# One PSUM bank for each evicting engine in the layer norm's transposes of an eight-core transformer and expert layer

## The chip, the cores and the metric

The kernel runs on the 8 cores of one Trainium2 chip. Each core does the whole program on a sequence of 2048 tokens of its own, with the same weights, and the cores exchange nothing. The time is the device time of the slowest core in microseconds (us), as a median of several runs.

## What is computed

The input is 8 x 2048 x 1024 in float32, 1024 being the width. Four transformer blocks run in turn, each with a layer norm, an attention half and a second layer norm with an FFN of width 4096. Of the eight heads four attend in windows of 128 tokens, and four are causal linear attention in buckets of 64. After them comes a sum with the input, a plain layer norm, and a dense mixture of 64 experts of width 512 with a shared one, then a last layer norm.

```python
for i in range(DEPTH):                       # 4
    x = x + self_attention(layer_norm(x, ln1_g[i], ln1_b[i]), Wq[i], Wk[i], Wv[i], Wo[i], bo[i])
    h = layer_norm(x, ln2_g[i], ln2_b[i])
    x = x + (gelu(h @ W1[i] + b1[i]) @ W2[i] + b2[i])
...
x = _layernorm(x0 + x)
shared = silu(xf @ Ws_up) @ Ws_down
h = silu(einsum('td,edf->etf', xf, W_up))
y = einsum('etf,efd->etd', h, W_down)
routed = einsum('etd,te->td', y, cw)         # cw: weights of the 8 chosen of 64 experts, else 0
out = _layernorm(x + shared + routed)
```

## The kernel before, in words

The activations stay in SBUF all the time: x_sb holds the 16 token blocks of 128 tokens by 1024 in float32. Matmuls want the activations transposed, with the width on the partitions. So each layer norm writes its result as bfloat16 into aT, transposed, and the stage behind it reads aT.

emit_ln makes one such layer norm. It is called nine times: two for each of the four blocks, and one before the experts. It has two parts. The first takes the variances of all 16 token blocks, ACT and DVE in turn (L308, L317), and then the square root and the reciprocal on small tiles. The second is a loop over the 16 token blocks. In it, one engine normalises a block from x_sb into one half of apre: ACT for even blocks (L352), DVE for odd ones (L356). In the ninth call the same engine writes x_sb too, in place (L363 on ACT, L367 on DVE). TensorE transposes the block in 8 pieces of 128 x 128 into PSUM (L379). ACT and DVE then carry the 8 pieces from PSUM to aT, which is called eviction here. They apply the norm's gain and offset on the way (L401 on ACT, L405 on DVE); the ninth call has none and copies (L396, L398). A piece fills a quarter kilobyte per partition, 8 fill one PSUM bank. Block b uses bank 6 for even b and bank 7 for odd b, and piece dt is evicted by ACT for even dt and by DVE for odd dt.

The order of work is that in which the Python code emits it: each engine has its own queue in that order, and semaphores between engines are set by hand. Each engine counts its marks on one semaphore: s_te for TensorE, s_act, s_dve. A Guard protects a buffer or a bank: use(eng) makes an engine wait for the last mark of every engine that has used it, its own too, and done(eng) records its mark. There is one Guard for each PSUM bank (gbank), one for aT (gaT), and those of apre (gapre and one for each eighth of it). A wait that the engine has already made for as high a count is left out.

Around the norms: before each norm the POOL queue waits for TensorE's last mark, and then issues the weight loads of the next stage as soon as their slots are free. emit_attention and emit_ffn start with a matmul that waits for aT_toks, the marks behind the last evictions. Banks 6 and 7 are used elsewhere only by attention, for small transposes (L655, L894). The other six banks (Pf) take the matmuls.

Of the kernel before, what the change touches and what calls it, by code (L numbers as in the profile page):

```python
# [38 lines left out]
class Eng:  # L39
    def __init__(self, bass_eng, sem, name):  # L40
        self.e = bass_eng
        self.sem = sem
        self.name = name
        self.count = 0
        self.waited = {}
        self.last_inst = None
        self.last_tok = None
# [71 lines left out]
class Guard:  # L119

    def __init__(self, prog):
        self.p = prog
        self.marks = {}

    def use(self, eng):
        for name, tok in list(self.marks.items()):
            self.p.wait(eng, tok)

    def done(self, eng):
        self.marks[eng.name] = eng.mark()  # L130

    def done_tok(self, name, tok):
        self.marks[name] = tok


def build_program(n_layers=DEPTH, do_top=True, do_moe=True, n_experts=NE,
# [31 lines left out]
    with ExitStack() as stack:  # L168
# [16 lines left out]
        te, act, dve, sp, gp = P.te, P.act, P.dve, P.sp, P.gp  # L185

        gbank = [Guard(P) for _ in range(8)]
# [20 lines left out]
        def stage_use_all(eng):  # L208
            gstage.use(eng)
            for n in SREGS:  # L210
                RG(n).use(eng)
# [6 lines left out]
        def apre_use_half(eng, half):  # L218
            gapre.use(eng)
            for i in range(4 * half, 4 * half + 4):  # L220
                apg(i).use(eng)

        def apre_done_half(eng, half):
            tok = eng.mark()
            gapre.done_tok(eng.name, tok)
            for i in range(4 * half, 4 * half + 4):
                apg(i).done_tok(eng.name, tok)
# [14 lines left out]
        def fpair(i, n=1024):  # L242
            return Pf[:, i * 512:i * 512 + n]

        def bbank(i, lo=0, hi=1024):
            return Pb[:, (i - 6) * 1024 + lo:(i - 6) * 1024 + hi]

        def sm(col, n=1):
            return smalls[:, col:col + n]

        def xt(t, lo=0, hi=1024):
            return x_sb[:, t * 1024 + lo:t * 1024 + hi]

        def aTv(dt, t0, t1):
            return aT[:, dt * T + t0:dt * T + t1]
# [41 lines left out]
        def emit_ln(gcol, bcol, sums_toks, inplace_nat=False, gb_toks=()):  # L297
            P.waits(dve, sums_toks)
            dve.emit(nc.vector.tensor_scalar(
                sm(NEGMU, NT), sm(SUMS, NT), -1.0 / D, None, op0=ALU.mult))  # L300
            negmu_tok = dve.mark()
            P.wait(act, negmu_tok)
            for t in range(NT):
                engv = act if t % 2 == 0 else dve
                if engv is act:
                    stage_use_all(engv)
                    P.wait(engv, xw_tok[t])
                    engv.emit(nc.scalar.activation(  # L308
                        stage[:], xt(t), AF.Square, bias=sm(NEGMU + t),
                        scale=1.0, accum_out=sm(VARSS + t)))  # L310
                    gstage.done(engv)
                else:
                    gbank[0].use(engv)
                    gbank[1].use(engv)
                    P.wait(engv, xw_tok[t])
                    P.wait(engv, negmu_tok)
                    engv.emit(nc.vector.scalar_tensor_tensor(  # L317
                        fpair(0), xt(t), sm(NEGMU + t), xt(t),
                        op0=ALU.add, op1=ALU.mult,
                        accum_out=sm(VARSS + t)))  # L320
                    gbank[0].done(engv)
                    gbank[1].done(engv)
            vs_tok = act.mark()
            P.wait(dve, vs_tok)
            P.selfbar(dve)
            dve.emit(nc.vector.tensor_scalar(
                sm(STD, NT), sm(VARSS, NT), 1.0 / D, 1e-5,
                op0=ALU.mult, op1=ALU.add))
            pre_tok = dve.mark()
            P.wait(act, pre_tok)  # L330
            act.emit(nc.scalar.activation(sm(STD, NT), sm(STD, NT), AF.Sqrt))
            std_tok = act.mark()
            P.wait(dve, std_tok)
            dve.emit(nc.vector.reciprocal(sm(RECR, NT), sm(STD, NT)))
            P.selfbar(dve)
            dve.emit(nc.vector.tensor_tensor(
                sm(MUR, NT), sm(NEGMU, NT), sm(RECR, NT), op=ALU.mult))
            mur_tok = dve.mark()

            aT_toks = []  # L340
            tr_prev = {6: None, 7: None}
            for b in range(NT):
                t = b
                pb = 6 + (b % 2)
                half = b % 2
                ap0 = half * 1024
                neng = act if b % 2 == 0 else dve
                apre_use_half(neng, half)
                P.wait(neng, mur_tok)
                P.wait(neng, xw_tok[t])  # L350
                if neng is act:
                    neng.emit(nc.scalar.activation(  # L352
                        apre[:, ap0:ap0 + 1024], xt(t), AF.Identity,
                        bias=sm(MUR + t), scale=sm(RECR + t)))
                else:
                    neng.emit(nc.vector.tensor_scalar(  # L356
                        apre[:, ap0:ap0 + 1024], xt(t),
                        sm(NEGMU + t), sm(RECR + t),
                        op0=ALU.add, op1=ALU.mult))
                if inplace_nat:  # L360
                    P.selfbar(neng)
                    if neng is act:
                        neng.emit(nc.scalar.activation(  # L363
                            xt(t), xt(t), AF.Identity,
                            bias=sm(MUR + t), scale=sm(RECR + t)))
                    else:
                        neng.emit(nc.vector.tensor_scalar(  # L367
                            xt(t), xt(t), sm(NEGMU + t), sm(RECR + t),
                            op0=ALU.add, op1=ALU.mult))
                    xw_tok[t] = neng.mark()  # L370
                apre_done_half(neng, half)
                norm_tok = neng.mark()
                g = gbank[pb]
                g.use(te)
                apre_use_half(te, half)
                P.wait(te, norm_tok)
                P.wait(te, tok_cst)
                for dt in range(8):
                    te.emit(nc.tensor.transpose(  # L379
                        bbank(pb, dt * 128, (dt + 1) * 128),  # L380
                        apre[:, ap0 + dt * 128:ap0 + (dt + 1) * 128],
                        ident))
                g.done(te)
                apre_done_half(te, half)
                tr_tok = te.mark()
                for dt in range(8):
                    eng = act if dt % 2 == 0 else dve
                    g.use(eng)
                    gaT.use(eng)
                    P.wait(eng, tr_tok)  # L390
                    P.waits(eng, gb_toks)
                    src = bbank(pb, dt * 128, dt * 128 + 128)
                    dst = aTv(dt, t * 128, (t + 1) * 128)
                    if gcol is None:
                        if eng is act:
                            eng.emit(nc.scalar.copy(dst, src))  # L396
                        else:
                            eng.emit(nc.vector.tensor_copy(dst, src))  # L398
                    else:
                        if eng is act:  # L400
                            eng.emit(nc.scalar.activation(  # L401
                                dst, src, AF.Identity,
                                bias=sm(bcol + dt), scale=sm(gcol + dt)))
                        else:
                            eng.emit(nc.vector.tensor_scalar(  # L405
                                dst, src, sm(gcol + dt), sm(bcol + dt),
                                op0=ALU.mult, op1=ALU.add))
                    g.done(eng)
                aT_toks.append(act.mark())
                aT_toks.append(dve.mark())  # L410
            return aT_toks
# [787 lines left out]
        if do_top:  # L1199
# [26 lines left out]
            if do_moe:  # L1226
                cw_toks = []
                for t in range(NT):
                    pb = 2 + t % 2
                    g = gbank[pb]  # L1230
# [50 lines left out]
                for idx, eix in enumerate(ex_list):  # L1281
# [8 lines left out]
                    for fs in range(4):  # L1290
                        for tc in range(4):
                            pb = (fs * 4 + tc) % 2
                            g = gbank[pb]
# [24 lines left out]
                    for t in range(NT):  # L1318
# [8 lines left out]
                        for half in range(2):  # L1327
                            pbk = pair + half
# [186 lines left out]
```

How the kernel before makes its waits and increments, by code:

```python
    def mark(self):  # L49
        if self.last_tok is not None:
            return self.last_tok
        if self.last_inst is None:
            return None
        try:
            self.last_inst.then_inc(self.sem, 1)
        except Exception:
            self.e.maybe_drain_then_inc((self.sem, 1))
        self.count += 1
        self.last_tok = (self.sem, self.count, self)
        return self.last_tok
# [25 lines left out]
    def wait(self, eng, tok):  # L86
        if tok is None:
            return
        sem, val, owner = tok
        key = id(sem)
        if eng.waited.get(key, -1) >= val:
            return
        eng.e.wait_ge(sem, val)
        eng.waited[key] = val
# [8 lines left out]
    def dma(self, queue_eng, kind, out_ap, in_ap, deps=()):  # L103
# [4 lines left out]
        sem = pool["sems"][idx]  # L108
        prior = pool["uses"][idx]
        if prior:
            self.wait(queue_eng, (sem, 16 * prior, None))
        inst = queue_eng.e.dma_start(out_ap, in_ap)
        inst.then_inc(sem, 16)
        pool["uses"][idx] = prior + 1
        queue_eng.emit(inst)
# [20 lines left out]
def build_program(n_layers=DEPTH, do_top=True, do_moe=True, n_experts=NE,  # L136
# [1305 lines left out]
                P.dma(sp, "o", xvv, xv)  # L1442
            elif tn == "qkvA":
                P.dma(sp, "o", ap, qkvA[:])
            elif tn == "smalls":
                P.dma(sp, "o", ap, smalls[:])
        for kind in ("w", "x", "o"):
            pool = P.pools[kind]
            for sem, uses in zip(pool["sems"], pool["uses"]):
                if uses:
                    sp.e.wait_ge(sem, 16 * uses)
    return nc
```

## Time and profile before

| what | value |
|---|---|
| median of the 3 runs | 9803.64 us (9411.13 to 10576.59) |
| time of the profiled execution | 9405.97 us |
| its span (slowest core) | 9404.9 us; all cores 9392.5 to 9404.9 |
| PE busy | 7248.0 us, 77% of the span |
| DVE busy | 3433.5 us, 37% |
| ACT busy | 2298.1 us, 24% |
| granted TensorE clock, mean | 0.859 to 0.861 on all cores |

The span runs from the first to the last instruction of one profiled execution. Busy time is the sum of an engine's instructions. A released instruction shows, in square brackets, how long its engine stood idle before it and whose end let it go. The granted clock is a share of 2.4 GHz: 0.50 is 1.2 GHz.

### The profile page before, as it was taken

The page shows a single profiled execution, that of the slowest core. Times are in us where ns is not written, and L with a number is a line of the kernel's source. Part 1 is how long each engine was busy: PE and PEld are TensorE (multiplying, and loading weights), DVE is VectorE, ACT ScalarE, POOL GpSimd, SP SyncE. Part 2 cuts the span into 40 slices and gives each one's busy share as a digit, 9 for nine tenths or more (in the row PEclk, how much of TensorE's full clock was granted, in tenths as well). Part 3 has the DMA queues.
Part 4 walks back from the last instruction along what each step waited for, and adds up shares of the span by engine and source line. Part 5 has one row for each costly group of instructions (what it writes and reads, how often), then busy time and mean ns, then how long its engine had stood idle before and what let it go on. Part 6 is the DMA issues. An engine that isn't in the chain of part 4 may idle for free.

```text
span 9404.9 us, 113236 instructions; the slowest of 8 cores (9392.5 to 9404.9 us)
## 1 busy us (share of the span) xinstructions
PE 7248.0 (77%) x36528; PEld 3413.1 (36%) x36528; DVE 3433.5 (37%) x6712; ACT 2298.1 (24%) x5374; POOL 223.8 (2%) x275
## 2 busy tenths in 40 slices
PE   2555994565966557955559919999999999999996
PEld 1342432332423433423424314444444444444442
DVE  3443333432334333334433333333333333333333
ACT  2343223333123332233432121111111111111112
POOL 0000000000000000000000000000000000000000
PEclk9666996667987668976569959999999999999998
DMA  3001211001210011211012112222222222222221
GB/s 59 8 8 18 36 26 16 10 6 29 39 21 10 12 19 23 32 18 13 8 21 36 29 41 36 36 37 40 36 36 40 37 36 37 41 36 36 40 37 45
DMA packets 234511, 269.89 MB, mean 29 GB/s; under 512 B 41824, under 2 KB 174048, under 8 KB 233952
## 3 DMA queue, kind: packets, MB, share of 16 engines
q0 software_dynamic: 224112, 237.14, 16.9%
q1 hardware_dynamic: 9840, 25.51, 0.8%
q8 instruction: 325, 5.32, 0.2%
q14 instruction: 234, 1.92, 0.1%
HBM read 491.36 MB, written 8.39 MB: 53 GB/s over the span
## 4 chain that ended last, share of the span: by engine, by line
PE 72%; DVE 9%; ACT 8%; issue 7%; DMA 2%; DVEq 1%; ACTq 0%; SPq 0%; POOLq 0%
PE Pf L1330 19%; PE Pf L1300 19%; PE Pf L1138 9%; PE Pf L1103 9%; PE Pf L1051 3%; ACT aT L401 3%; PE Pf L533 2%; PE Pf L851 2%; DVE aT L405 2%; PE Pf L500 2%; PE Pb L379 2%; PE Pf L790 2%; DVE stage L609 1%; ACT apre L884 1%; ACT apre L352 1%
## 5 line engine op out<-in xcount | busy, mean ns | idle before, releaser
L1353 DVE SCALAR_TENSOR_TENSOR x_sb<-Pf,smalls,x_sb 128x1024 f32<-128x1024 f32 x1024 | 1314.1, 1283 | 2320.0 <-PE Pf L1330 2318.2
L1330 PE MATMUL Pf<-wA,bigB 128*128 128x512 bf16 x8320 | 1826.5, 378 | 68.4 <-ACT bigB L1309 65.0
L1300 PE MATMUL Pf<-aT,wA 128*128 128x512 bf16 x8320 | 1808.2, 379 | 1.0 <-ACT bigB L1309 1.0
L1309 ACT ACTIVATE bigB<-Pf 128x512 bf16<-128x512 f32 x1040 | 620.8, 597 | 3038.9 <-PE Pf L1300 3038.9
L1300 PEld LDWEIGHTS Pf<-aT,wA 128*128 128x128 bf16 x8320 | 814.4, 98 | 983.8 <-issue 3.6
L1330 PEld LDWEIGHTS Pf<-wA,bigB 128*128 128x128 bf16 x8320 | 744.7, 97 | 1150.2 <-issue 393.1
L1138 PE MATMUL Pf<-wA,bigB 128*128 128x512 bf16 x4096 | 911.8, 379 | 36.1 <-ACT bigB L1114 34.9
L1165 DVE TENSOR_TENSOR x_sb<-Pf,x_sb 128x1024 f32<-128x1024 f32 x448 | 548.6, 1225 | 1052.3 <-PE Pf L1138 1051.2
L1103 PE MATMUL Pf<-aT,wA 128*128 128x512 bf16 x4096 | 897.0, 381 | 19.3 <-DVE aT L405 17.9
L379 PE MATMUL Pb<-constsB,apre 128*128 128x128 bf16 x1152 | 145.7, 307 | 993.8 <-ACT apre L352 477.9
L1114 ACT ACTIVATE bigB<-Pf,smalls 128x512 bf16<-128x512 f32 x512 | 351.5, 687 | 1337.2 <-PE Pf L1103 1337.2
L1103 PEld LDWEIGHTS Pf<-aT,wA 128*128 128x128 bf16 x4096 | 401.9, 98 | 508.9 <-issue 31.3
L1138 PEld LDWEIGHTS Pf<-wA,bigB 128*128 128x128 bf16 x4096 | 369.5, 97 | 545.6 <-issue 189.6
L379 PEld LDWEIGHTS Pb<-constsB,apre 128*128 128x128 bf16 x1152 | 111.5, 138 | 1027.9 <-issue 1027.9
L405 DVE TENSOR_SCALAR aT<-Pb,smalls 128x128 bf16<-128x128 bf16 x512 | 176.0, 344 | 569.7 <-ACT aT L401 569.7
L401 ACT ACTIVATE aT<-Pb,smalls 128x128 bf16<-128x128 bf16 x512 | 234.1, 457 | 479.8 <-PE Pb L379 248.2
L894 PE MATMUL Pb<-constsB,apre 128*128 128x128 bf16 x256 | 66.4, 259 | 310.3 <-ACT apre L884 310.3
L655 PE MATMUL Pb<-constsB,apre 128*128 128x128 bf16 x496 | 88.6, 277 | 266.5 <-DVE smalls L637 244.5
L500 PE MATMUL Pf<-wA,aT 128*128 128x256 bf16 x2048 | 278.5, 289 | 19.9 <-DVE aT L405 17.9
L1051 PE MATMUL Pf<-wA,bigB 128*128 128x512 bf16 x1024 | 251.5, 390 | 2.4 <-ACT bigB L968 2.4
L851 PE MATMUL Pf<-wA,aT 128*128 128x128 bf16 x2048 | 231.9, 302 | 27.5 <-DMA wA<-Wq 27.5
L790 PE MATMUL Pf<-wA,aT 128*128 128x256 bf16 x1024 | 178.1, 333 | 96.6 <-DVE qkvA L817 75.0
(122 smaller groups left out, 4829.4 us busy)
## 6 DMA issues: line engine op xcount, KB each, us to landing
wA<-W POOLq DMA_DIRECT2D x64, 1024.0 KB, 10.5
wA<-Wup POOLq DMA_DIRECT2D x64, 1024.0 KB, 10.8
wA<-Wdn POOLq DMA_DIRECT2D x64, 1024.0 KB, 9.8
x_sb<-x SPq DMA_DIRECT2D x1, 8192.0 KB, 35.3
wA<-Wv POOLq DMA_DIRECT2D x16, 512.0 KB, 7.6
wA<-Wo POOLq DMA_DIRECT2D x4, 2048.0 KB, 27.0
stage<-x SPq DMA_DIRECT2D x16, 512.0 KB, 3.5
out<-stage SPq DMA_DIRECT2D x16, 512.0 KB, 2.6
```

The source lines that it names most:

```text
L379: te.emit(nc.tensor.transpose(bbank(pb, dt * 128, (dt + 1) * 128), apre[:, ap0 + dt * 128:ap0 + (dt + 1) * 128], ident))
L401: eng.emit(nc.scalar.activation(dst, src, AF.Identity, bias=sm(bcol + dt), scale=sm(gcol + dt)))
L500: te.emit(nc.tensor.matmul(fbank(pb, 0, 256), aTv(dt, t * 128, (t + 1) * 128), wv(base + dt * 256, 256), start=(dt == 0), stop=(dt == 7)))
L851: te.emit(nc.tensor.matmul(fbank(pb, 0, 128), aTv(dt, t * 128, (t + 1) * 128), wv(qbase + dt * 256 + hh * 128, 128), start=(dt == 0), stop ...
L1051: te.emit(nc.tensor.matmul(fbank(pbk), oTv(et, t * 128, (t + 1) * 128), wv(6144 + et * 1024 + half * 512, 512), start=(et == 0), stop=False))
L1103: te.emit(nc.tensor.matmul(fbank(pb), wv(par * 4096 + dt * 512 + fs * 128, 128), aTv(dt, tc * 512, (tc + 1) * 512), start=(dt == 0), stop= ...
L1138: te.emit(nc.tensor.matmul(fbank(pbk), bigB[:, par * 8192 + fs * 2048 + t * 128: par * 8192 + fs * 2048 + (t + 1) * 128], wv(8192 + par * ...
L1165: dve.emit(nc.vector.tensor_tensor(xt(t), fpair(pair), xt(t), op=ALU.add))
L1300: te.emit(nc.tensor.matmul(fbank(pb), wv(par * 4096 + dt * 512 + fs * 128, 128), aTv(dt, tc * 512, (tc + 1) * 512), start=(dt == 0), stop= ...
L1309: act.emit(nc.scalar.activation(bigB[:, par * 8192 + fs * 2048 + tc * 512: par * 8192 + fs * 2048 + (tc + 1) * 512], fbank(pb), AF.Silu))
L1330: te.emit(nc.tensor.matmul(fbank(pbk), bigB[:, par * 8192 + fs * 2048 + t * 128: par * 8192 + fs * 2048 + (t + 1) * 128], wv(8192 + par * ...
L1353: dve.emit(nc.vector.scalar_tensor_tensor(xt(t), fpair(pair), sm(CW + t * 64 + eix), xt(t), op0=ALU.mult, op1=ALU.add, **kw))
```

## The change

The second part of emit_ln changes. Each token block now uses both banks: pieces 0 to 3 go into bank 6 and are all evicted by ACT, pieces 4 to 7 go into bank 7 and are all evicted by DVE. Each bank has the Guard it had. TensorE uses both Guards before a block's transposes and marks both behind them, and an evicting engine uses only the Guard of its own bank. The class Guard also gets a second kind of use, for readers, with use_r and done_r; no call of these two is in the kernel.

```diff
@@ class Guard
         self.marks = {}
+        self.readers = {}
 
     def use(self, eng):
-        for name, tok in list(self.marks.items()):
+        for tok in list(self.marks.values()):
+            self.p.wait(eng, tok)
+        for tok in list(self.readers.values()):
             self.p.wait(eng, tok)
 
     def done(self, eng):
         self.marks[eng.name] = eng.mark()
+        self.readers.clear()
...
@@ emit_ln
-                g = gbank[pb]
-                g.use(te)
+                g6 = gbank[6]
+                g7 = gbank[7]
+                g6.use(te)
+                g7.use(te)
                 apre_use_half(te, half)
                 P.wait(te, norm_tok)
                 P.wait(te, tok_cst)
                 for dt in range(8):
+                    pbk = 6 + (dt >= 4)
                     te.emit(nc.tensor.transpose(
-                        bbank(pb, dt * 128, (dt + 1) * 128),
+                        bbank(pbk, (dt % 4) * 128, (dt % 4 + 1) * 128),
                         apre[:, ap0 + dt * 128:ap0 + (dt + 1) * 128],
                         ident))
-                g.done(te)
+                g6.done(te)
+                g7.done(te)
                 apre_done_half(te, half)
                 tr_tok = te.mark()
                 for dt in range(8):
-                    eng = act if dt % 2 == 0 else dve
+                    eng = act if dt < 4 else dve
+                    g = g6 if dt < 4 else g7
                     g.use(eng)
                     gaT.use(eng)
                     P.wait(eng, tr_tok)
                     P.waits(eng, gb_toks)
-                    src = bbank(pb, dt * 128, dt * 128 + 128)
+                    src = bbank(6 + (dt >= 4), (dt % 4) * 128,
+                                (dt % 4) * 128 + 128)
                     dst = aTv(dt, t * 128, (t + 1) * 128)
```

No engine gets another instruction or another order of them; the waits change. The first place is DVE in the first norm, from the evictions of block 0 through the normalisation of block 1 to its evictions. L405 is the eviction, L356 the normalisation; each row ends with the semaphores that its instruction waits for. Before:

```order
L405 TENSOR_SCALAR aT<-Pb,smalls 128x128 [waits s_te,s_act,s_xdma3,s_xdma4]
L405 TENSOR_SCALAR aT<-Pb,smalls 128x128 [waits s_act,s_dve] x3
L356 TENSOR_SCALAR apre<-x_sb,smalls 128x1024
L405 TENSOR_SCALAR aT<-Pb,smalls 128x128 [waits s_te,s_act]
L405 TENSOR_SCALAR aT<-Pb,smalls 128x128 [waits s_act,s_dve] x3
```

The same place on DVE after the change, where the two lines are L423 and L368:

```order
L423 TENSOR_SCALAR aT<-Pb,smalls 128x128 [waits s_te,s_xdma3,s_xdma4]
L423 TENSOR_SCALAR aT<-Pb,smalls 128x128 [waits s_dve] x3
L368 TENSOR_SCALAR apre<-x_sb,smalls 128x1024 [waits s_act]
L423 TENSOR_SCALAR aT<-Pb,smalls 128x128 [waits s_te,s_dve]
L423 TENSOR_SCALAR aT<-Pb,smalls 128x128 [waits s_dve] x3
```

The wait for ACT has left the evictions, and one for ACT stands at the normalisation, where there was none; on ACT's queue the same holds the other way round.

The second place is PE at the transposes of the first three token blocks. Before:

```order
L379 MATMUL Pb<-constsB,apre 128x128 [waits barrier_Pool_Activation_PE_DVE_SP_release,s_act,s_xdma0]
L379 MATMUL Pb<-constsB,apre 128x128 x7
L379 MATMUL Pb<-constsB,apre 128x128 [waits s_te,s_dve]
L379 MATMUL Pb<-constsB,apre 128x128 x7
L379 MATMUL Pb<-constsB,apre 128x128 [waits s_act,s_te]
```

After, where the line is L394:

```order
L394 MATMUL Pb<-constsB,apre 128x128 [waits barrier_Pool_Activation_PE_DVE_SP_release,s_act,s_xdma0]
L394 MATMUL Pb<-constsB,apre 128x128 x7
L394 MATMUL Pb<-constsB,apre 128x128 [waits s_te,s_act,s_dve]
L394 MATMUL Pb<-constsB,apre 128x128 x7
L394 MATMUL Pb<-constsB,apre 128x128 [waits s_te,s_act,s_dve]
```

From the second block on, the first transpose waits for both ACT and DVE, where it waited for one of them in turn.

## Rows read from the trace of the kernel before

**Rows 1.** The page, busy tenths of PE in 40 equal slices of the span.

```profile
PE   2555994565966557955559919999999999999996
```

**Rows 2.** The page, groups by line: busy us, mean ns | idle before, releaser.

```profile
L405 DVE TENSOR_SCALAR aT<-Pb,smalls 128x128 bf16<-128x128 bf16 x512 | 176.0, 344 | 569.7 <-ACT aT L401 569.7
L401 ACT ACTIVATE aT<-Pb,smalls 128x128 bf16<-128x128 bf16 x512 | 234.1, 457 | 479.8 <-PE Pb L379 248.2
```

**Rows 3.** Line L379: idle time of PE before it, by what ended it (us, times).

```profile
  ACT apre L352: 477.9, 64
  DVE apre L356: 330.6, 64
  ACT x_sb L363: 147.6, 8
  DVE x_sb L367: 37.7, 8
```

**Rows 4.** Timeline, two token blocks of the second norm: start us, us, instruction [idle <-releaser].

```profile
839.47 1.01 PE L379 MATMUL Pb<-constsB,apre 128*128 128x128 bf16 x8 [5.08 <-ACT apre L352]
840.58 0.46 ACT L401 ACTIVATE aT<-Pb,smalls 128x128 bf16<-128x128 bf16 x1 [1.36 <-PE Pb L379]
...
841.58 0.46 ACT L401 ACTIVATE aT<-Pb,smalls 128x128 bf16<-128x128 bf16 x1 [0.54 <-DVE aT L405]
842.21 0.34 DVE L405 TENSOR_SCALAR aT<-Pb,smalls 128x128 bf16<-128x128 bf16 x1 [0.73 <-ACT aT L401]
842.65 0.46 ACT L401 ACTIVATE aT<-Pb,smalls 128x128 bf16<-128x128 bf16 x1 [0.61 <-DVE aT L405]
...
844.35 0.34 DVE L405 TENSOR_SCALAR aT<-Pb,smalls 128x128 bf16<-128x128 bf16 x1 [0.73 <-ACT aT L401]
844.61 0.80 DVE L356 TENSOR_SCALAR apre<-x_sb,smalls 128x1024 bf16<-128x1024 f32 x1
...
845.56 1.01 PE L379 MATMUL Pb<-constsB,apre 128*128 128x128 bf16 x8 [5.08 <-DVE apre L356]
...
849.81 0.46 ACT L401 ACTIVATE aT<-Pb,smalls 128x128 bf16<-128x128 bf16 x1 [0.61 <-DVE aT L405]
850.17 1.23 ACT L352 ACTIVATE apre<-x_sb,smalls 128x1024 bf16<-128x1024 f32 x1
...
851.65 1.01 PE L379 MATMUL Pb<-constsB,apre 128*128 128x128 bf16 x8 [5.08 <-ACT apre L352]
```

**Rows 5.** Timeline, PE's first matmuls of the FFN behind that norm.

```profile
924.17 2.29 PE L1103 MATMUL Pf<-aT,wA 128*128 128x512 bf16 x5 [4.47 <-DVE aT L405]
```

**Rows 6.** Timeline, linear attention: DVE waits for itself, ACT reads PSUM beside it.

```profile
456.50 0.28 DVE L979 TENSOR_TENSOR stage<-Pf,stage 128x129 f32<-128x129 f32 x1
456.51 0.21 ACT L968 CAST bigB<-Pf 128x64 bf16<-128x64 f32 x1 [0.61 <-PE Pf L957]
...
456.88 0.15 DVE L983 TENSOR_SCALAR smalls<-stage 128x1 f32<-128x1 f32 x1
```

**Rows 7.** Line L979, all its instructions: min/median/max ns, first and last start.

```profile
L979 DVE TENSOR_TENSOR stage<-Pf,stage x496: 272/293/296, 406.0 to 4733.7; 128x129 f32<-128x129 f32 x166
```

**Rows 8.** Timeline, one token block of the ninth norm.

```profile
5507.55 0.27 ACT L396 COPY aT<-Pb 128x128 bf16<-128x128 bf16 x1 [3.29 <-PE Pb L379]
...
5509.72 0.27 ACT L396 COPY aT<-Pb 128x128 bf16<-128x128 bf16 x1 [0.48 <-DVE aT L398]
5509.88 1.24 ACT L352 ACTIVATE apre<-x_sb,smalls 128x1024 bf16<-128x1024 f32 x1
5510.16 0.23 DVE L398 COPY aT<-Pb 128x128 bf16<-128x128 bf16 x1 [0.52 <-ACT aT L396]
5511.22 1.24 ACT L363 ACTIVATE x_sb<-x_sb,smalls 128x1024 f32<-128x1024 f32 x1
```

**Rows 9.** DMA from 811 to 925: busy tenths of the 16 engines in 40 slices.

```profile
DMA  1999999997400000000000000000000000000000
```

**Rows 10.** Busy us (x) of PE, PEld, DVE, ACT, POOL, PEclk, DMA share, GB/s, second norm.

```profile
829.00:918.00 89.00, 14.16 (x112) 10.85 (x112) 25.80 (x68) 34.86 (x66) 0.00 (x0) 0.50 0.14 22
```

More of the change, by code:

```diff
@@ L130, in done, with use_r, done_r @@
         self.marks[eng.name] = eng.mark()
+        self.readers.clear()
     def done_tok(self, name, tok):
         self.marks[name] = tok
+        self.readers.clear()
+    def use_r(self, eng):
+        for tok in list(self.marks.values()):
+            self.p.wait(eng, tok)
+    def done_r(self, eng):
+        self.readers[eng.name] = eng.mark()
 def build_program(n_layers=DEPTH, do_top=True, do_moe=True, n_experts=NE,
```

## The prediction

> **What bounds the kernel now.** Begin with how busy TensorE is along the span [rows 1]. PE is at 9 tenths in the expert stage and in the four FFN stages, and low between them. In some of the low slices it does next to nothing: these hold the layer norms, nine in all. Then the groups by line [rows 2]. The two lines that carry a transposed tile from PSUM to aT, L401 on ACT and L405 on DVE, run 512 times each. DVE stood idle 569.7 us before its own, all of it waiting for ACT, and ACT 479.8 us before its own. What ended PE's idle time before the transposes (L379) is in [rows 3]: a normalisation on ACT (L352) or DVE (L356), or the in-place pair L363/L367 of the ninth norm, 993.8 us in all; never an eviction. So the layer norm is one chain: normalise a block, transpose it, evict it, normalise the next.
>
> The timeline of two blocks shows the chain [rows 4]. From one group of transposes to the next it is 6.09 us (839.47, 845.56, 851.65), of which PE works 1.01. The evictions go ACT, DVE, ACT, DVE, each started by the end of the other's: ACT 841.58, DVE 842.21, ACT 842.65, so 1.07 us for each pair, four pairs a block. They don't share data; they share a bank, and the guard of that bank makes each wait for the mark of the last. The first matmul of the FFN waits for the norm's last eviction [rows 5], and by the code that of attention does so too, so what a norm loses or gains goes to the end one for one. The span is 9404.9 us and the execution's own time 9405.97; the sum is made against the latter. It is 4.1% under the median of the runs shown (9803.64) and 0.05% under the lowest (9411.13), so what I give is the time of a run like the profiled one.
>
> **The change, part by part.** Guard: nothing ever fills the new dictionary of readers, so the new loop and the clears issue nothing: 0. Transposes: the same 8 per block, 4 into each bank, still released together: 0. Evictions: the same 8 with the same shapes and time (0.457 and 0.344), but ACT takes the first four from bank 6 and DVE the last four from bank 7. Each chain then waits only for its own engine. This is the term.
>
> How long is a step when an engine waits for its own last instruction? On DVE, L983 waits so for L979 [rows 6]: 456.50 + 0.28 to 456.88, a gap of 0.10. On ACT, L363 waits so for L352 [rows 8]: 5509.88 + 1.24 to 5511.22, again 0.10. So I take 0.56 for a step on ACT (0.457 + 0.10) and 0.45 on DVE (0.344 + 0.10, rounded up). The trace shows no such wait between two evictions, so this needs bounds. Below, it is no exposed gap, as where L352 starts 0.36 after the last L401 and L356 0.26 after the last L405 [rows 4]: 0.36 and 0.26. Above, the bound is today's pair, 1.07 for either. The value is near the lower end because the own-engine rows are the nearest.
>
> Do they slow each other, now that they read PSUM at one time? In [rows 6] L979 on DVE and L968 on ACT, both reading Pf, start 0.01 us apart; this L979 takes 0.28, and all 496 of them take 0.272 to 0.296 [rows 7], whether or not ACT reads beside them. I charge 0.
>
> Now the blocks, from the start of the transposes. Where DVE normalises next (from 839.47) [rows 4]: 1.11 to the first eviction; three DVE steps of 0.45; 0.26 to L356; 0.95 to the next transposes: 3.67, against 6.09, saves 2.42. The transposes now need both banks, so ACT must be done too: 1.11 + 3 x 0.56 + 0.46 = 3.25, which is 0.42 before 3.67. Where ACT normalises next (from 845.56) [rows 4]: 1.11; three ACT steps, 1.68; 0.36 to L352; 1.48 to the transposes: 4.63, against 6.09, saves 1.46. Last block: its evictions end 3.25 after the start of its transposes, against 5.22 now (839.47 to 844.35 + 0.34), saves 1.97. A norm has 16 blocks: eight intervals of the first kind, seven of the second and the end: 19.36 + 10.22 + 1.97 = 31.6. Eight such norms: 252.4 us.
>
> The ninth norm [rows 8] copies in 0.27 on ACT and 0.23 on DVE: steps of 0.37 and 0.33. What comes before the first eviction and after the last stays, so differences do. From the first eviction to DVE's last it is 2.61 (5507.55 to 5510.16) and becomes 0.99: saves 1.62 where DVE goes on. To ACT's last it is 2.17 and becomes 1.11: saves 1.06 where ACT goes on. To the end 2.84, becomes 1.11 + 0.27: saves 1.46. Together 12.96 + 7.42 + 1.46 = 21.8 us.
>
> Two waits are new. The normalisation on DVE waits for ACT's semaphore, which the order shows. By the code it is the mark of ACT's normalisation one block before, and that stands on ACT ahead of the evictions: long past, 0. Behind it on DVE would stand the four evictions of its own block, and PE waits for them all. The other is PE's wait for both banks, priced above: covered by 0.42 us; if an ACT step grew beyond 0.70 that cover would be gone.
>
> What is late next? Weights: in the norm from 811 to 925 the DMA engines are busy in the first 11 of 40 slices, to about 842 [rows 9]; the norm now ends at 924 and would end at 892. 50 us of cover stay. After each norm PE starts as before. The clock granted in this norm is 0.50, the 1.2 GHz level [rows 10], and eight transposes take 1.01. I leave it so.
>
> Sum: 252.4 + 21.8 = 274.2; 9405.97 - 274.2 = **9132 us**, 2.9% less.
>
> A rule speaks against this change. The Trainium skill, Perfetto Trace Analysis, section Optimizing Tensor Performance (Matmuls), wants independent groups to rotate through different banks, so that the eviction of one overlaps the next group's work on TensorE; the kernel before does that and the changed one stops. In this trace the rotation buys nothing: PE never waited for an eviction here, since what it waited for, the normalisation, itself stands behind evictions on its engine [rows 3, 4]. By the rule, the sum would be that of the second rival.
>
> **Rivals.**
> (1) The steps are longer than an own-engine wait makes them, as with two engines reading PSUM in step. At 0.20 more for each step (0.76 and 0.65) a pair of blocks loses 1.2 of its 3.88 us; 72 pairs, 86 us: 9218. At the upper bound of 1.07 the first kind is 5.53, the second 6.16, the end 4.78: 8 x 0.56 - 7 x 0.07 + 0.44 = 4.4 us a norm, 40 us in all: 9366. Against it: [rows 6].
> (2) The rotation of banks was worth something. If transposes had run beside the last block's evictions, 1.01 and the 0.10 behind it would come into the open, 1.1 x 135 intervals = 150 us: 9282. For it: there are two halves of apre and two banks. Against it: 1.01 us already stands in the open in each block [rows 4].
> (3) The new wait of DVE's normalisation is for ACT's last eviction after all. Then it starts at 3.25 + 0.10, not 2.72: 0.63 on 72 intervals, 45 us: 9177. For it: the order shows a wait that was not there. Against it: the code.
> (4) The clock rises in the norms, as transposes come every 4.15 us, not 6.09. At 2.4 GHz the 1.01 halves: 0.5 x 144 = 72 us: 9060. Against it: PE is still idle three quarters of the time.
> (5) Slower: ACT and DVE hold each other up on PSUM at each eviction. A pair of blocks is then 5.27 + 6 steps against 12.18 today, so the change loses from a mean step of 1.15 us, and is 2% slower from 1.59. At four times the present ACT eviction, 1.83, a pair takes 16.25; 4.07 x 72 = 293: 9699. For it: no row has these two lines side by side. Against it: the reads of [rows 6].
>
> **How the numbers follow.** A measurement of this kernel tells about 2% from no change, 188 us. Forecast 0.78; (1) mild 0.05, strong 0.04; (2) 0.02; (3) 0.04; (4) 0.05; (5) 0.02. All but strong (1), (2) and (5) end below 9218, the edge of 2%, or at it; half of mild (1) is put under same. So faster 0.89, same 0.09, slower 0.02. The lower bounds of the steps (0.36, 0.26) give 1.17 more a pair, 84 us: 9048. The range is 9060 to 9230: the forecast with most of the way to that lower bound, (3), mild (1), and (4) at its edge.
>
> **What would show it.** In the timeline of a norm: four ACT evictions 0.56 apart beside four of DVE 0.45 apart; transposes 3.67 and 4.63 apart in turn; idle time before DVE's evictions ended by PE, not ACT; a norm of 97 us of blocks down to 65. Wrong it would be if steps came at 0.7 or more (rivals 1 and 5), if PE's wait named an eviction (2), if L356's named ACT (3), if eight transposes took 0.5 (4), or if the norms shrank as said and the time did not.

## The result

The changed kernel is faster. The ratio of its time to that of the kernel before is 0.9714, 95% interval 0.969 to 0.9737; the forecast of 9132 us against 9405.97 us is a ratio of 0.9709. The lowest times are 9134.68 us (9 runs) and 9404.69 us (10 runs), the medians 9822.97 and 9665.51 us. In most executions, of either kernel, the cores of one or both dies ran at a lower granted clock and took up to an eighth longer, so the ratio leaves such runs out, and every time below is that of the slowest core of a die at its usual clock.

The two kernels by that measure:

| kernel | slowest core of a die, us | dies | median |
|---|---|---|---|
| before | 9404.7 to 9412.3 | 19 | 9407 |
| changed | 9130.1 to 9140.2 | 13 | 9134 |

The rows of after are those of core 4 (granted clock 0.869 in the mean, 0.860 before). First the groups by line, which answer to [rows 2]; L419 and L423 are now the evictions on ACT and DVE, L394 the transposes (busy us, mean ns | idle before, releasers):

```profile
L419 ACT ACTIVATE aT<-Pb,smalls 128x128 bf16<-128x128 bf16 x512 | 234.2, 458 | 229.2 <-PE Pb L394 191.8 <-ACT aT L419 1.9
L423 DVE TENSOR_SCALAR aT<-Pb,smalls 128x128 bf16<-128x128 bf16 x512 | 175.7, 343 | 311.5 <-PE Pb L394 269.3 <-DVE aT L423 0.9
```

The evictions take what they took, 458 and 343 ns against 457 and 344, though they now run side by side. Their idle time has fallen by about half, from 479.8 to 229.2 us on ACT and from 569.7 to 311.5 us on DVE. PE now ends most of it (191.8 and 269.3 us), where ACT had ended all of DVE's. What PE waited for before the transposes, against [rows 3]:

```profile
  ACT apre L364: 391.6, 64
  DVE apre L368: 178.3, 64
  ACT x_sb L375: 137.3, 8
  DVE x_sb L379: 25.6, 8
```

Again normalisations only, now 732.8 us for 993.8. PE has lost 261 us of idle time here. The timeline of two blocks of the second norm, against [rows 4] (start us, us, instruction [idle <-releaser]; "x4" is four instructions drawn as one):

```profile
794.75 1.01 PE L394 MATMUL Pb<-constsB,apre 128*128 128x128 bf16 x8 [3.54 <-ACT apre L364]
795.92 2.11 ACT L419 ACTIVATE aT<-Pb,smalls 128x128 bf16<-128x128 bf16 x4 [1.31 <-PE Pb L394]
795.94 1.70 DVE L423 TENSOR_SCALAR aT<-Pb,smalls 128x128 bf16<-128x128 bf16 x4 [2.85 <-PE Pb L394]
797.56 0.80 DVE L368 TENSOR_SCALAR apre<-x_sb,smalls 128x1024 bf16<-128x1024 f32 x1
...
798.51 1.01 PE L394 MATMUL Pb<-constsB,apre 128*128 128x128 bf16 x8 [2.75 <-DVE apre L368]
799.67 2.11 ACT L419 ACTIVATE aT<-Pb,smalls 128x128 bf16<-128x128 bf16 x4 [1.65 <-PE Pb L394]
...
801.69 1.23 ACT L364 ACTIVATE apre<-x_sb,smalls 128x1024 bf16<-128x1024 f32 x1
...
803.06 1.01 PE L394 MATMUL Pb<-constsB,apre 128*128 128x128 bf16 x8 [3.54 <-ACT apre L364]
```

Four evictions on ACT last 2.11 us, so a step is (2.11 - 0.46) / 3 = 0.55; on DVE (1.70 - 0.34) / 3 = 0.45. The transposes stand 3.76 and 4.55 us apart, not twice 6.09. Behind the norm the FFN follows as it did, against [rows 5]:

```profile
852.28 1.01 PE L1121 MATMUL Pf<-aT,wA 128*128 128x512 bf16 x2 [2.62 <-ACT aT L419]
```

This norm took 81.7 us from its first instruction to here (770.56 to 852.28), 113.0 before (811.22 to 924.17). All nine, so measured, took 743.7 us where they took 1020.3: 276.6 us less, 31.0 to 32.5 in each of the first eight and 22.4 in the ninth. The stages between them changed by 9.0 us together, of which 10.2 in the first attention stage alone. That stage takes 635.1 to 643.2 us on the eight cores of the kernel before, so this part is within what cores differ by and isn't shown to come from the change. With 1.0 us more at the start that is the 284.5 us between the spans of core 4 (9404.9 and 9120.4). Busy us of PE, PEld, DVE and ACT, granted clock, DMA share and GB/s of the norm and the FFN behind it:

```profile
770.56:852.28 81.72, 16.18 (x129) 12.41 (x129) 39.33 (x92) 49.86 (x90) 2.35 (x3) 0.52 0.33 52
852.28:1322.25 469.97, 458.85 (x2080) 195.68 (x2080) 156.85 (x144) 89.14 (x129) 10.80 (x14) 1.00 0.17 28
```

The clock in the norm is at the 1.2 GHz level as before, and eight transposes still take 1.01 us. The FFN takes 470.0 us, before 469.5.

### The profile page after: what moved, and what is told of

Read it like the earlier page. It is cut to its first block, busy times and chain, and to the rows that moved or that the text cites. A ratio compares the mean times of both kernels' runs of the same rounds, so it can differ in the third digit from the quotient of the medians.

```text
span 9377.4 us, 112200 instructions; the slowest of 8 cores (9120.4 to 9377.4 us)
## 1 busy us (share of the span) xinstructions
PE 7456.1 (80%) x35971; PEld 3494.2 (37%) x36528; DVE 3435.0 (37%) x6712; ACT 2302.0 (25%) x5374; POOL 224.2 (2%) x275
## 4 chain that ended last, share of the span: by engine, by line
PE 75%; DVE 8%; issue 7%; ACT 7%; DMA 2%; DVEq 0%; ACTq 0%; SPq 0%; POOLq 0%
PE Pf L1318 20%; PE Pf L1348 20%; PE Pf L1156 9%; PE Pf L1121 9%; PE Pf L1069 2%; PE Pf L551 2%; PE Pf L869 2%; PE Pf L808 2%; PE Pf L518 2%; PE Pb L394 2%; DVE stage L627 1%; ACT aT L419 1%; ACT apre L902 1%; ACT apre L364 1%; DVE Pf L329 1%
## 5 line engine op out<-in xcount | busy, mean ns | idle before, releaser
L1348 PE MATMUL Pf<-wA,bigB 128*128 128x512 bf16 x8153 | 1933.3, 397 | 79.6 <-ACT bigB L1327 65.6
L1318 PE MATMUL Pf<-aT,wA 128*128 128x512 bf16 x8154 | 1922.6, 398 | 10.8 <-issue 0.2
L1348 PEld LDWEIGHTS Pf<-wA,bigB 128*128 128x128 bf16 x8320 | 794.7, 101 | 1218.2 <-issue 703.8
L1318 PEld LDWEIGHTS Pf<-aT,wA 128*128 128x128 bf16 x8320 | 843.6, 101 | 1079.2 <-issue 413.7
L1156 PE MATMUL Pf<-wA,bigB 128*128 128x512 bf16 x4012 | 905.4, 379 | 42.3 <-ACT bigB L1132 35.2
L1121 PE MATMUL Pf<-aT,wA 128*128 128x512 bf16 x4012 | 890.9, 381 | 18.2 <-ACT aT L419 12.3
L394 PE MATMUL Pb<-constsB,apre 128*128 128x128 bf16 x1152 | 145.7, 307 | 735.8 <-ACT apre L364 390.9
L1121 PEld LDWEIGHTS Pf<-aT,wA 128*128 128x128 bf16 x4096 | 401.9, 98 | 501.7 <-issue 24.3
L1156 PEld LDWEIGHTS Pf<-wA,bigB 128*128 128x128 bf16 x4096 | 369.4, 97 | 546.2 <-issue 190.4
L394 PEld LDWEIGHTS Pb<-constsB,apre 128*128 128x128 bf16 x1152 | 111.5, 138 | 769.9 <-issue 769.9
L419 ACT ACTIVATE aT<-Pb,smalls 128x128 bf16<-128x128 bf16 x512 | 234.4, 458 | 229.3 <-PE Pb L394 192.0
L423 DVE TENSOR_SCALAR aT<-Pb,smalls 128x128 bf16<-128x128 bf16 x512 | 176.2, 344 | 311.6 <-PE Pb L394 269.4
L1069 PE MATMUL Pf<-wA,bigB 128*128 128x512 bf16 x1000 | 246.7, 387 | 5.1 <-ACT bigB L986 4.2
```

Of the source, the lines that this page charges most:

```text
L394: te.emit(nc.tensor.transpose(bbank(pbk, (dt % 4) * 128, (dt % 4 + 1) * 128), apre[:, ap0 + dt * 128:ap0 + (dt + 1) * 128], ident))
L1069: te.emit(nc.tensor.matmul(fbank(pbk), oTv(et, t * 128, (t + 1) * 128), wv(6144 + et * 1024 + half * 512, 512), start=(et == 0), stop=False))
L1121: te.emit(nc.tensor.matmul(fbank(pb), wv(par * 4096 + dt * 512 + fs * 128, 128), aTv(dt, tc * 512, (tc + 1) * 512), start=(dt == 0), stop= ...
L1156: te.emit(nc.tensor.matmul(fbank(pbk), bigB[:, par * 8192 + fs * 2048 + t * 128: par * 8192 + fs * 2048 + (t + 1) * 128], wv(8192 + par * ...
L1318: te.emit(nc.tensor.matmul(fbank(pb), wv(par * 4096 + dt * 512 + fs * 128, 128), aTv(dt, tc * 512, (tc + 1) * 512), start=(dt == 0), stop= ...
L1348: te.emit(nc.tensor.matmul(fbank(pbk), bigB[:, par * 8192 + fs * 2048 + t * 128: par * 8192 + fs * 2048 + (t + 1) * 128], wv(8192 + par * ...
```

## The experiments

Theory: the norm is one chain of normalisation, transposes and evictions. The evictions' part of it shrank because each engine now waits only for itself, and the two engines work at one time. Its rivals are that the layout in two banks is what counts, that the handovers between engines are, and that the lost rotation of banks costs something.

**Two banks, alternation kept.**

```diff
-                for dt in range(8):
+                for dt in (0, 4, 1, 5, 2, 6, 3, 7):
                     eng = act if dt < 4 else dve
                     g = g6 if dt < 4 else g7
-                    g.use(eng)
+                    g6.use(eng)
+                    g7.use(eng)
```

> The changed kernel with its two banks, but the eight evictions taken in turn again (pieces 0, 4, 1, 5, 2, 6, 3, 7) and each waiting for the guards of both banks. Theory (the gain is the alternation of waits that went, not the layout): the pairs come every 1.07 us again, transposes every 6.1 us, a norm's blocks take 97 us, and the time is that of the kernel before, 9406 us. Rival (two banks themselves make evictions or transposes quicker): it stays near the changed kernel, 9135 us, or lands in between.

Measured: 9426.8 to 9430.7 us on three dies, and 9431.74 as the time of one undisturbed run. The timeline of a block of this kernel (L420 and L424 are its evictions):

```profile
838.95 1.01 PE L394 MATMUL Pb<-constsB,apre 128*128 128x128 bf16 x8 [5.27 <-DVE apre L368]
840.17 0.46 ACT L420 ACTIVATE aT<-Pb,smalls 128x128 bf16<-128x128 bf16 x1 [2.60 <-PE Pb L394]
840.80 0.34 DVE L424 TENSOR_SCALAR aT<-Pb,smalls 128x128 bf16<-128x128 bf16 x1 [2.00 <-ACT aT L420]
841.24 0.46 ACT L420 ACTIVATE aT<-Pb,smalls 128x128 bf16<-128x128 bf16 x1 [0.61 <-DVE aT L424]
...
845.11 1.01 PE L394 MATMUL Pb<-constsB,apre 128*128 128x128 bf16 x8 [5.15 <-ACT apre L364]
```

The pairs are back at 1.07 us (840.17 to 841.24), and with them the whole gain is gone. The layout in two banks alone is worth nothing. It is even 20 us slower than the kernel before, which I had not expected: the first eviction comes 1.22 us after the start of the transposes and not 1.11, and DVE's first 0.17 after ACT's end (840.63) and not 0.10.

**One bank, no rotation.**

```diff
-                pb = 6 + (b % 2)
+                pb = 6
```

> The kernel before with bank 6 for every token block, so the rotation of banks is gone and the alternation of the evictions stays. Theory (the rotation bought nothing, as the normalisation already stands behind the evictions): 6.1 us per block as before, 9406 us. Rival (the rotation was worth 1.1 us a block, which the changed kernel pays): 7.2 us per block, 1.1 x 135 = 150 us more, 9556 us.

Measured: 9426.9 to 9429.5 us on four dies. The rival's 9556 is out. So is the forecast of no difference at all: these are the same 20 us as above, with the same 0.11 and 0.07 (844.33 + 1.22, and 846.01 to 846.19 in the next rows, its L401 and L405):

```profile
844.33 1.01 PE L379 MATMUL Pb<-constsB,apre 128*128 128x128 bf16 x8 [5.26 <-DVE apre L356]
845.55 0.46 ACT L401 ACTIVATE aT<-Pb,smalls 128x128 bf16<-128x128 bf16 x1 [2.60 <-PE Pb L379]
846.19 0.34 DVE L405 TENSOR_SCALAR aT<-Pb,smalls 128x128 bf16<-128x128 bf16 x1 [2.00 <-ACT aT L401]
```

The order of instructions shows what both kernels have in common: their first evictions wait for s_te, s_act and s_dve in that order, where those of the kernel before wait for s_te alone on ACT, and for s_te and s_act on DVE. The wait that ends last is not the last in the list. This was tried further below.

**One handover a block.** In the kernel before:

```diff
-                    eng = act if dt % 2 == 0 else dve
+                    eng = act if dt < 4 else dve
```

> The kernel before, its bank rotation kept, but ACT evicts pieces 0 to 3 and DVE then pieces 4 to 7 of the same bank: one handover a block in place of seven, and still no two evictions at one time. Theory (side by side is where most of the gain is; own-engine steps are 0.56 and 0.45): where DVE normalises next 1.16 + 2.14 + 0.17 + 1.35 + 0.26 + 0.95 = 6.0 us; where ACT normalises next it goes on beside DVE's evictions, 4.6 us; 8 x 0.1 + 7 x 1.5 + 0.1 = 11 us a norm, about 95 in all: 9310 us. Rival (the handovers were the cost, not the serial order): near 9135 us.

Measured: 9296.9 to 9298.3 us on three dies. Timeline of two blocks:

```profile
822.77 1.01 PE L379 MATMUL Pb<-constsB,apre 128*128 128x128 bf16 x8 [4.88 <-DVE apre L356]
823.94 2.11 ACT L401 ACTIVATE aT<-Pb,smalls 128x128 bf16<-128x128 bf16 x4 [3.84 <-PE Pb L379]
825.95 1.23 ACT L352 ACTIVATE apre<-x_sb,smalls 128x1024 bf16<-128x1024 f32 x1
826.15 1.70 DVE L405 TENSOR_SCALAR aT<-Pb,smalls 128x128 bf16<-128x128 bf16 x4 [3.53 <-ACT aT L401]
827.43 1.01 PE L379 MATMUL Pb<-constsB,apre 128*128 128x128 bf16 x8 [3.64 <-ACT apre L352]
828.54 2.11 ACT L401 ACTIVATE aT<-Pb,smalls 128x128 bf16<-128x128 bf16 x4 [1.36 <-PE Pb L379]
...
833.32 0.90 PE L379 MATMUL Pb<-constsB,apre 128*128 128x128 bf16 x7 [4.88 <-DVE apre L356]
```

Forecast 6.0 and 4.6 us, measured 5.89 and 4.66. Handovers fell from seven to one and four tenths of the gain came (110 of 273 us). Most of that is not the handovers: where ACT normalises next (L352 at 825.95) it does so beside DVE's evictions, and the transposes at 827.43, of an even block, write bank 6 while DVE still reads bank 7. The rest of the gain came with the two engines evicting at one time, which the change does from two banks. Whether two banks are needed for that isn't shown: evictions at one time from the same bank weren't tried, as the guard is there to keep them apart.

**No own wait at the evictions.** In the changed kernel:

```diff
                     g = g6 if dt < 4 else g7
-                    g.use(eng)
```

> The changed kernel, the evictions without the wait for their own engine's last mark (each engine keeps its order). Theory (a step is the instruction plus 0.10 because of that wait, and 0.10 less than the instruction without it): four evictions start 0.36 apart on ACT and 0.26 on DVE; transposes 3.2 and 4.0 us apart where they are 3.75 and 4.55; 1.14 us a pair of blocks, 82 us: 9050 us. Rival (both engines on PSUM set the step, or the drain stays): 9135 us.

Measured: 9034.0 and 9034.9 us on two dies, 99 us under the changed kernel where 82 was expected. Its timeline is that of core 0 (L418 and L422 are the evictions). That core's granted clock was 0.766 over its whole span, but 0.50 in this norm as in the others, and eight transposes take the same 1.01 us:

```profile
798.92 1.01 PE L394 MATMUL Pb<-constsB,apre 128*128 128x128 bf16 x8 [2.88 <-ACT apre L364]
800.03 1.50 ACT L418 ACTIVATE aT<-Pb,smalls 128x128 bf16<-128x128 bf16 x4 [1.26 <-PE Pb L394]
800.04 1.10 DVE L422 TENSOR_SCALAR aT<-Pb,smalls 128x128 bf16<-128x128 bf16 x4 [2.79 <-PE Pb L394]
...
802.01 1.01 PE L394 MATMUL Pb<-constsB,apre 128*128 128x128 bf16 x8 [2.08 <-DVE apre L368]
...
805.90 0.37 PE L394 MATMUL Pb<-constsB,apre 128*128 128x128 bf16 x2 [2.88 <-ACT apre L364]
```

Steps of 0.35 and 0.25, transposes 3.09 and 3.89 apart: 1.33 us a pair, of which 1.2 are the six steps. The other 0.13 is the first eviction, at 1.11 again with one wait in its list. The wait for the own mark is as dear as the prediction bounded it from below: 0.20 us a step.

**Normalisation ahead of the evictions.** In the changed kernel the normalisation becomes a function, norm_block, called one block ahead (the lines behind the dots are in it):

```diff
                 tr_tok = te.mark()
+                if b + 1 < NT:
+                    norm_next = norm_block(b + 1)
                 for dt in range(8):
                     eng = act if dt < 4 else dve
...
+                if b < 2:
+                    apre_use_half(neng, half)
+                else:
+                    for i in range(4 * half, 4 * half + 4):
+                        apg(i).use(neng)
```

> The changed kernel with the normalisation of block b+1 put ahead of the evictions of block b in its engine's queue (from the third block on without the wait that covers both halves of apre), so that it runs beside the transposes of block b. Theory (one chain through normalisation, transposes and evictions): the normalisation leaves the chain, and PE's wait for both banks ends last, named as an eviction by ACT: 1.17 + 2.11 + 0.1 = 3.4 us from one group of transposes to the next, in place of 3.75 and 4.55; 11 us a norm, some 24 in the ninth, 112 in all: 9023 us. Rival (the chain has another member than these three, or the norms run beside other work): less than 30 us, above 9105 us.

> The same, and the evictions without the wait for their own engine's last mark. Theory: 1.11 + 1.50 + 0.1 = 2.7 us from one group of transposes to the next; 22 us a norm less than the changed kernel, 28 in the ninth, 205 in all: 8930 us. Rival (ACT's work becomes the bound, two blocks of evictions and one normalisation with what lies between): 3.2 us a block and 9000 us.

Measured, with the own wait 9037.3 to 9041.0 us on four dies, and without it 8935.0 to 8940.8 on five. The timelines, first with the own wait:

```profile
800.12 1.01 PE L404 MATMUL Pb<-constsB,apre 128*128 128x128 bf16 x8 [2.51 <-ACT aT L431]
801.29 2.11 ACT L431 ACTIVATE aT<-Pb,smalls 128x128 bf16<-128x128 bf16 x4 [1.42 <-PE Pb L404]
...
803.29 1.23 ACT L367 ACTIVATE apre<-x_sb,smalls 128x1024 bf16<-128x1024 f32 x1
803.64 1.01 PE L404 MATMUL Pb<-constsB,apre 128*128 128x128 bf16 x8 [2.51 <-ACT aT L431]
```

and without it:

```profile
801.73 1.01 PE L404 MATMUL Pb<-constsB,apre 128*128 128x128 bf16 x8 [1.85 <-ACT aT L430]
802.84 1.50 ACT L430 ACTIVATE aT<-Pb,smalls 128x128 bf16<-128x128 bf16 x4 [0.23 <-PE Pb L404]
...
804.59 1.01 PE L404 MATMUL Pb<-constsB,apre 128*128 128x128 bf16 x8 [1.85 <-ACT aT L430]
```

Blocks come every 3.52 and 2.86 us (3.4 and 2.7 forecast), and PE's wait names an eviction by ACT in both, which it never did in the kernel before or the changed one. What the forecasts had too small is the last term: the transposes start 0.25 us after the end of ACT's last eviction (803.40 to 803.64), not 0.1. Only now is the bank what PE waits for; whether a second pair of banks would help wasn't tried.

**Both, and each bank handed over by itself.** In the kernel with both edits:

```diff
-                g7.use(te)
...
                 for dt in range(8):
                     pbk = 6 + (dt >= 4)
+                    if dt == 4:
+                        g6.done(te)
+                        tr6_tok = te.mark()
+                        g7.use(te)
...
-                    P.wait(eng, tr_tok)
+                    P.wait(eng, tr6_tok if dt < 4 else tr_tok)
```

> As the kernel with both edits (normalisation ahead, no own waits), and each bank handed over by itself: PE waits for bank 7 only before the fifth transpose, and marks bank 6 behind the fourth, so that ACT starts half a microsecond sooner. Theory: ACT's own work is now the bound, four evictions of 1.50 and a normalisation of 1.23 in turn: transposes 2.2 and 2.65 us apart in turn, 5 us less a norm, 40 in all: 8890 us. Rival (PE's order ties the two banks together): no gain on the kernel with both edits.

Measured: 8888.7 to 8893.6 us on five dies, 2.7% under the changed kernel and 5.5% under the one before. Timeline (L432 and L436 evict, L367 and L371 normalise):

```profile
776.13 1.01 PE L407 MATMUL Pb<-constsB,apre 128*128 128x128 bf16 x8 [1.56 <-DVE aT L436]
776.82 1.50 ACT L432 ACTIVATE aT<-Pb,smalls 128x128 bf16<-128x128 bf16 x4
...
778.57 1.01 PE L407 MATMUL Pb<-constsB,apre 128*128 128x128 bf16 x8 [1.43 <-ACT aT L432]
779.26 1.51 ACT L432 ACTIVATE aT<-Pb,smalls 128x128 bf16<-128x128 bf16 x4 [0.93 <-PE Pb L407]
...
780.64 1.25 ACT L367 ACTIVATE apre<-x_sb,smalls 128x1024 bf16<-128x1024 f32 x1
...
781.12 1.01 PE L407 MATMUL Pb<-constsB,apre 128*128 128x128 bf16 x8 [1.53 <-DVE aT L436]
781.80 1.51 ACT L432 ACTIVATE aT<-Pb,smalls 128x128 bf16<-128x128 bf16 x4
```

The transposes are 2.44 and 2.55 us apart (2.2 and 2.65 forecast), 4.99 for two blocks. The time was met, but not by the mechanism I gave. ACT's own work for two blocks is two times 1.50 and 1.23, 4.23 us, and ACT stands idle 0.93 us before its evictions at 779.26, until PE releases it. The normalisation that stands before the evictions at 781.80 doesn't delay them either: they start 0.68 us after the transposes, as the others do (0.69). What sets the pace is a ring over bank 6: 0.69 us from the start of the transposes to ACT's first eviction, 1.50 of evictions, and 0.25 or 0.36 from their end to the next transposes (778.32 to 778.57, 780.76 to 781.12). DVE is named before the transposes at 781.12 because its mark came last, 0.04 us behind ACT's. By the trace it held nothing up: PE was still going through its waits one by one, s_act at 780.80, s_te at 780.91, s_dve at 781.01. The table of waits further below has what each of them takes.

**The order of two waits.** The waits that an engine has to make before an instruction are its wait list here. In the changed kernel:

```diff
                     g = g6 if dt < 4 else g7
+                    P.wait(eng, g.marks.get(eng.name))
                     g.use(eng)
```

> The changed kernel with nothing but the order of two waits turned at the first eviction of a block: that for the engine's own mark, long passed, stands ahead of that for the transposes. Theory (the first eviction came 1.17 us after the start of the transposes and not 1.11, as the wait that ends last stands first in the list and the other is then gone through behind it): 1.11 and 1.11, 0.06 to 0.08 a block, about 10 us: 9125 us. Rival (the 0.06 is the cost of any second wait, or of both engines being released by one mark): the first eviction stays at 1.17 and the time at 9135 us.

Measured: 9125.2 to 9127.5 us on three dies, 8 us under the changed kernel. Both engines' first evictions come at 1.11 and 1.12:

```profile
794.47 1.01 PE L394 MATMUL Pb<-constsB,apre 128*128 128x128 bf16 x8 [3.48 <-ACT apre L364]
795.58 2.11 ACT L420 ACTIVATE aT<-Pb,smalls 128x128 bf16<-128x128 bf16 x4 [1.25 <-PE Pb L394]
795.59 1.70 DVE L424 TENSOR_SCALAR aT<-Pb,smalls 128x128 bf16<-128x128 bf16 x4 [2.79 <-PE Pb L394]
```

Eight us are near what dies differ by (9130.1 to 9140.2), so the rows carry this, not the time. The same on the kernel before, at every eviction, where it counts three more times a block:

```diff
                     eng = act if dt % 2 == 0 else dve
+                    P.wait(eng, g.marks.get(eng.name))
+                    if dt == 0:
+                        P.wait(eng, g.marks.get("dve"))
                     g.use(eng)
```

> The kernel before, rotation and alternation kept, only the order of the waits at an eviction turned: the engine's own mark, long passed, first, and the one that ends last at the end of the list. Theory (a wait that ends last costs 0.07 us more where another stands behind it): the handover from ACT to DVE goes from 0.17 to 0.10, three times a block, so pairs every 1.00 us and not 1.07, and 5.88 us per block: 0.21 x 144 = 30 us: 9378 us. Rival (0.17 against 0.10 is what the two engines differ by): 9408 us.

And the same again with bank 6 alone:

> The same with bank 6 for every token block. Theory (the rotation bought nothing; the 20 us of the kernel with one bank came from the order of its waits): 5.88 us per block and 9378 us, the time of its sibling with two banks in rotation. Rival (the rotation was worth 0.13 us a block in itself): 6.0 us per block and 9398 us.

Measured: 9375.9 to 9383.4 us on six dies with rotation, and 9373.5 to 9382.9 on six without. The timeline of the kernel with one bank (L404 and L408 evict):

```profile
846.22 1.01 PE L379 MATMUL Pb<-constsB,apre 128*128 128x128 bf16 x8 [5.51 <-DVE apre L356]
847.33 0.46 ACT L404 ACTIVATE aT<-Pb,smalls 128x128 bf16<-128x128 bf16 x1 [2.43 <-PE Pb L379]
847.89 0.34 DVE L408 TENSOR_SCALAR aT<-Pb,smalls 128x128 bf16<-128x128 bf16 x1 [1.82 <-ACT aT L404]
848.33 0.46 ACT L404 ACTIVATE aT<-Pb,smalls 128x128 bf16<-128x128 bf16 x1 [0.54 <-DVE aT L408]
...
852.06 1.01 PE L379 MATMUL Pb<-constsB,apre 128*128 128x128 bf16 x8 [4.83 <-ACT apre L352]
```

A pair takes 1.00 us, the first eviction comes at 1.11, and the two kernels agree in time. So the rotation of banks was worth nothing here, and the 20 us of the kernel with one bank were the order of its waits.

**What the traces show of the lists.** No kernel turned waits on PE, but the traces hold the waits themselves. Each is an instruction of its own on its engine (EVENT_SEMAPHORE at L93, which the timeline leaves out), and an engine goes through them one after the other. The table has the median us from the last mark waited for (an instruction's mark is counted 0.01 us behind its end) to the start of the instruction, over the waits that ended more than 0.4 us of idle time, on one core of each kernel:

| engine | nothing behind that wait | one wait behind it | two behind it |
|---|---|---|---|
| PE | 0.135 | 0.241 | 0.347 |
| ACT | 0.083 | 0.138 | 0.194 |
| DVE | 0.092 | 0.161 | |

The kernels agree within 0.003 us, but for the last PE column in the two with the normalisation ahead, whose 15 cases aren't alike. So a wait behind the one that ends last costs 0.11 us on PE, 0.055 on ACT and 0.07 on DVE. The same figures give the 0.25 us before PE's transposes above (s_act ends last and s_dve stands behind it), and the 0.36 with two waits behind.

## Why the prediction was right and where it failed

**The time given.** The range of 9060 to 9230 us doesn't hold the median of the runs, 9822.97. The step that failed is the first term of the sum, the base of 9405.97 us. I took it from the profiled execution, and put the 4.1% between it and the median shown (9803.64, with a run at 10576.59) at nothing: there is no term for it in the sum and no width for it in the range. The runs showed 9665.51 us as the median of the kernel before and 9822.97 as that of the changed one, 691 us above the forecast. The excess isn't in the norms. Core 0 of the changed kernel's profile has a span 257 us longer than core 4's, while its nine norms take 745.8 us against 743.7; 243 us of it lie behind the ninth norm, at a granted clock of 0.92 against 0.98, for a reason that stays open. The other term of the sum held: 273 us where 274.2 were forecast, and a ratio of 0.9714 for 0.9709.

**The chain and who ends it.** Right: [rows 3] named normalisations only, the rows after do too, and the kernel that puts the alternation back on two banks lost all of the gain.

**Steps of 0.56 and 0.45.** Measured 0.55 and 0.45. The lower bounds, 0.36 and 0.26, are what the evictions take without the own wait (0.35 and 0.25). The nearest rows, two chains of own waits on other instructions, were the right ones to take.

**Reads side by side cost nothing.** Right: 458 and 343 ns.

**Intervals of 3.67 and 4.63.** Measured 3.76 and 4.55. The sum of the two is right to 0.01, by two errors. The first eviction comes 1.17 to 1.19 us after the start of the transposes and not 1.11, as its wait list changed; that was not in the working, which took the 1.11 from [rows 4] though the order showed a second semaphore on those rows. That alone would have cost 0.13 us a pair of blocks, 9 us in all. And from ACT's normalisation to the next transposes it takes 1.37 and not 1.48. There PE's list was s_act, s_te, with s_act ending last and one wait behind it. It is now s_te, s_act, s_dve and once more s_act (the order in the change section names each semaphore once), with nothing behind the one that ends last. The table's 0.241 and 0.135 are this 0.11. Two terms that I took over unchanged from the rows had changed, in opposite directions; that they cancel is luck.

**A norm of 31.6 us less, 21.8 in the ninth.** Measured 31.0 to 32.5, and 22.4.

**The two new waits are free.** Right: DVE's normalisation starts 0.26 us after the start of its last eviction (797.30 to 797.56), and PE's wait for both banks never ended last. Rival (3) is out by this.

**The rotation.** The kernels with the turned waits show it at 0, with one bank and with two. The Trainium skill (Perfetto Trace Analysis, Optimizing Tensor Performance) wants it for the overlap of one group's eviction with the next group's work on TensorE. The kernel before had the banks for such an overlap and its queues didn't allow one. The kernel with one handover a block has it: there PE writes bank 6 while DVE reads bank 7 (827.43 to 827.85).

**The clock.** It stayed at the 1.2 GHz level in the norms, with transposes 4.15 us apart in the mean. Rival (4) is out.

## What to carry to other kernels

Where two engines empty one buffer in turn and the profile shows each idle for the other, ask whether they share data or only a guard: a bank and a guard of its own for each engine took 273 us of 9407 without a transpose or an eviction less. Then follow the chain on. Three things were worth another 244 us here (9134 to 8890): a wait for an engine's own last mark where nothing needs it, a step that sits in a queue behind work it doesn't depend on, and a bank that is handed over only together with another. Last, look at the order of the waits: the one that will end last belongs at the end of its list.

## What the runs showed of the hardware

- A wait for the engine's own last mark costs 0.20 us a step on ACT and DVE with 128x128 evictions: 0.55 with it and 0.35 without on ACT, 0.45 and 0.25 on DVE, 0.10 of each as an exposed gap and 0.10 as lost overlap.
- The order in a list of waits counts. An instruction starts later when the wait that ends last has another, long passed, behind it: by 0.055 us on ACT, 0.07 on DVE and 0.11 on PE. In the timelines that is 0.17 against 0.10 us from ACT's end to DVE's start, and 1.17 against 1.11 for the first eviction (1.22 with two waits behind). On ACT and DVE turning the order was tried and took it away; on PE it is read from the lists as they stand.
- The engine that the profile names before an instruction is the one whose mark came last, and need not be the one that held it: with bank 6 and bank 7 handed over one by one, PE started 0.25 us after ACT's end where one wait stood behind, and 0.36 where two did and DVE was named.
- ACT and DVE read PSUM from different banks at one time at full speed: 458 and 343 ns for the evictions side by side, 457 and 344 alone.
